# Softmax sums of the second layer's attention: quarters added by DMA, one product with ones per pair of heads

## The chip, the cores and the metric

The kernel runs on one core of one Trainium2 chip. The metric is device time in microseconds (us), the median of the runs shown; lower is better.

## The reference

Two transformer-like layers over 8 rows of 512 tokens with 128 features, all in float32. The change touches the attention of the second layer: 16 query heads of width 64 share one key and one value head.

```python
# x: (8, 512, 128), after the second layernorm
q = (x @ Wq + bq).reshape(B, S, H, DK)            # H = 16, DK = 64
k = x @ Wk + bk
v = x @ Wv + bv
scores = einsum('bshd,btd->bhst', q, k) / sqrt(DK)
w = softmax(scores, axis=-1)                      # over the 512 keys
out = einsum('bhst,btd->bshd', w, v).reshape(B, S, H * DV)
attn = out @ Wo + bo
```

Beside it stand, for each row, a first layer (an attention without softmax, and a feed-forward layer quantised to 4 bits) and a mixture of 8 experts, two for each token.

## The kernel before, in words

The program is written engine by engine, each with its own instruction list and explicit semaphores. The order comes from one list of steps, `steps`, which every engine walks. A row of the input is 64 steps of kind "o": a step is one head's scores against one quarter (128) of the keys, for all 512 queries. Heads go in pairs: eight steps make a pair, with the two heads in turn (steps 0 and 1: quarter 0 of both heads; 2 and 3: quarter 1; and so on), so a row has 8 pairs and the run 64. In the last row the 23 expert tiles (kind "ye") stand between them.

In one step TensorE (PE) makes the transposed scores with two products (`first`, L1438 and L1439) into one of two PSUM banks, and ScalarE (ACT) exponentiates them into one of the `WIDE = 6` buffers of `wide` (L846). `first` of step g waits for the exponential of step g - 2, and an exponential waits until the buffer of six steps ago has been used. Two steps after every fourth step `values` (L1449) takes four such buffers: eight products with the values (L1466), in four column tiles of 32 that run beside each other, and four with a matrix of ones (L1477), which add the weights over the 128 keys of a partition; a column tile is 32 output partitions. Float32 products are two instructions each in the trace, so a call of `values` is 16 instructions at L1466 and 8 at L1477. The last two pairs of the run are "direct": their sums are made on all 128 partitions and inverted from PSUM.

After a pair, ACT copies the values out of PSUM (`raw`, L872) and the sums (`sraw`, L877). SyncE (SP) stores the sums of the two heads and two halves to DRAM, loads them spread over 128 partitions (`sums`), VectorE (DVE) adds the two halves and inverts them (L1210), and SP stores the inverses and loads them spread over the partitions (`inv`, L500). DVE multiplies (L1223, at the steps in `NORM_AT`), and PE projects (L1498).

Around this the other work stands at fixed steps: per step DVE takes maxima of scores of pairs to come (L1029), PE makes those scores (L1392), DVE rounds queries (L1021), and the first layer of the next row runs by `L0_AT` and `L0_DVE`. The negated maxima reach the queries by a small DMA from ACT (L786), which the first scores of the next pair wait for. SP copies each pair's queries, SBUF to SBUF, with four DMAs (L537). GpSimd (POOL) has little to do in a row: three inverse roots for the layernorms (L636, each waits for DVE), the zeroing of the next row's slots in `x_rows` (L666) and the scattering of the row's tokens (L680, eight indirect DMAs).

Of the kernel before, what the change touches and what calls it, by code (L numbers as in the profile page):

```python
# [72 lines left out]
def two_layers(nc, a, out):  # L73
# [44 lines left out]
    WO_AT = [ATT - 10, ATT + 18]  # L118
# [6 lines left out]
    L0_DVE = [-14, -11, -11, -10, -7, -6, -4, -2, 0, 0, 9, 10, 13, 17, 18, 21, 25, 26, 29, 30, 30, 31, 32,  # L125
              34, 35, 37, 38, 39, 40, 42, 43, 44, 44]
# [9 lines left out]
    SPLIT_STEPS = [6 + 3 * j for j in range(2 * E)]  # L136

# [27 lines left out]

    def y_of(st):
        return HC * st.t + st.m
# [10 lines left out]
    def pair_end(st, after):  # L178

        past = behind(st, BEHIND + after)  # L180
        if past is None or past.kind != "o" or past.k % PAIR != PAIR - 1:
            return None
        return past.r * (H // 2) + past.k // PAIR

# [56 lines left out]
    def norm_at(r):  # L241

        at_ = dict(enumerate(NORM_AT))
# [57 lines left out]
    with ctx:  # L301
# [54 lines left out]
        part_h = sb("part_h", [P, PARTS, S], F32R)  # L356
# [10 lines left out]
        gcmp, geq = sb("gcmp", [P, TT * E, E]), sb("geq", [P, TT * E, E])  # L367
# [7 lines left out]
        tb_nt, tb_cum, tb_big = sb("tb_nt", [1, 2, E]), sb("tb_cum", [1, E]), sb("tb_big", [1, 2, TILES, E])  # L375
        tb_sq = sb("tb_sq", [1, E, E])
# [9 lines left out]
        zeros = part_h[:].rearrange("p n s -> p (n s)")[:, 0:TT * ROW].bitcast(F32)  # L386
# [15 lines left out]
        lo_done, second_done = sem("lo_done"), sem("second_done")  # L402
        out_free = [sem(f"out_free{i}") for i in range(OUTB)]
# [56 lines left out]
        def _(sp):  # L460
# [42 lines left out]
            def sums_and_inverses(r, k):  # L503
                for p in range(H // 2):
# [4 lines left out]
                    if k == PAIR * p + 12:  # L509
# [3 lines left out]
                        sp.dma_start(scratch_s[:, 2 * (p % 2):2 * (p % 2) + 2, :].rearrange("a b n -> b a n"), sraw[0:P:TILE, p % 2, :])\  # L513
                          .then_inc(sums_stored[p % 2], 16)
                    if k == PAIR * p + 12 and p % 2 == 1:
# [3 lines left out]
                        sp.dma_start(sums[:], scratch_s.rearrange("a g (p n) -> (g p) a n", p=32)).then_inc(sums_loaded, 16)  # L519
                    if k == PAIR * p + 17 and p % 2 == 1:  # L520
# [6 lines left out]
                        load_inverse(pair)  # L527

# [42 lines left out]
            for st in steps:  # L571
                for event in head_events(st):
# [39 lines left out]
        def _(pool):  # L612
# [44 lines left out]
            pool.memset(part_h[:].bitcast(F32), 0.0).then_inc(consts, 1)  # L657
# [3 lines left out]
            def zero(n):  # L661
                if n == 0:
                    pool.wait_ge(consts, N_CONSTS)
                    pool.dma_start(x_rows[E * ZONE:, :].rearrange("(p i) c -> p (i c)", p=P), zeros).then_inc(zeroed[0], 16)
                for e in range(E):
                    pool.dma_start(x_rows[ZONE * e + S * n:ZONE * e + S * (n + 1), :].rearrange("(p i) c -> p (i c)", p=P),  # L666
                                   zeros).then_inc(zeroed[n % 2], 16)

            def scatter(n):
                for b in range(2):  # L670
# [8 lines left out]
                    for i in range(TT):  # L679
                        pool.indirect_dma_start(x_rows, bass.IndirectOffsetOnAxis(ap=slot_u[:, b, i:i + 1], axis=0),  # L680
                                                xr[:, i, :], None).then_inc(scattered, 16)

            root()
            root()
            zero(0)
            zero(1)
            root()
            scatter(0)
            for j in range(2 * E):
                if SPLIT_STEPS[j] in (27, 45):  # L690
                    root()
# [4 lines left out]
            for n in range(1, NB):  # L696
                if n > 1:
                    root()
                    root()
# [887 lines left out]
```

## Time and profile before

| | us |
|---|---|
| median of 3 runs | 1349.38 (1345.81 to 1350.87) |
| profiled execution, its own time | 1346.94 |
| its span, first to last instruction | 1345.2 |

| engine | busy us | share |
|---|---|---|
| PE (matmul) | 1233.3 | 92% |
| DVE | 1011.2 | 75% |
| ACT | 683.2 | 51% |
| POOL | 263.2 | 20% |

The span has a beginning of 110 us, seven rows of second-layer attention from there to 1054.8 us, and the last row with the experts. Busy time of PE overlaps itself, since products run beside each other and their ends are modelled, so the chain of waits says more than the share. A line number (L1466) is one of the kernel before.

### The profile page before, as it was taken

The page shows a single profiled execution, that of the slowest core. Times are in us where ns is not written, and L with a number is a line of the kernel's source. Part 1 is how long each engine was busy: PE and PEld are TensorE (multiplying, and loading weights), DVE is VectorE, ACT ScalarE, POOL GpSimd, SP SyncE. Part 2 cuts the span into 40 slices and gives each one's busy share as a digit, 9 for nine tenths or more (in the row PEclk, how much of TensorE's full clock was granted, in tenths as well). Part 3 has the DMA queues.
Part 4 walks back from the last instruction along what each step waited for, and adds up shares of the span by engine and source line. Part 5 has one row for each costly group of instructions (what it writes and reads, how often), then busy time and mean ns, then how long its engine had stood idle before and what let it go on. Part 6 is the DMA issues. An engine that isn't in the chain of part 4 may idle for free.

```text
span 1345.2 us, 21825 instructions
## 1 busy us (share of the span) xinstructions
PE 1233.3 (92%) x7185; PEld 725.0 (54%) x7185; DVE 1011.2 (75%) x2393; ACT 683.2 (51%) x1252; POOL 263.2 (20%) x314
## 2 busy tenths in 40 slices
PE   4559999999999999999999999999999989998997
PEld 2335445554555455555555555455555458785843
DVE  7776888578857885788588857886796767686775
ACT  3126545544554455444644464446444468685741
POOL 2033222200120012001200120012000206372640
PEclk9659999999999999999999999999999999998998
DMA  2062665122312231224222321232121457474461
GB/s 78 0 174 69 193 200 179 49 63 56 115 36 63 65 116 38 52 67 100 64 50 55 115 65 50 49 120 65 50 50 49 131 173 232 153 238 137 150 214 55
DMA packets 89779, 133.80 MB, mean 99 GB/s; under 512 B 33293, under 2 KB 49229, under 8 KB 85701
## 3 DMA queue, kind: packets, MB, share of 16 engines
q1 hardware_dynamic: 75108, 99.80, 26.2%
q0 software_dynamic: 11344, 31.64, 7.1%
q8 instruction: 59, 0.97, 0.3%
q10 hardware_dynamic: 3216, 0.97, 0.3%
q14 instruction: 52, 0.42, 0.1%
HBM read 59.86 MB, written 38.68 MB: 73 GB/s over the span
## 4 chain that ended last, share of the span: by engine, by line
PE 69%; DVE 19%; issue 4%; ACT 3%; SPq 3%; DMA 2%; POOL 1%; DVEq 0%; ACTq 0%; POOLq 0%
PE bank L1466 14%; PE bank L1438 7%; PE bank L1477 6%; PE bank L1392 6%; PE bank L1439 5%; PE bank L1297 4%; PE bank L1498 4%; PE bank L1299 4%; PE bank L1298 4%; DVE mneg L1029 4%; DVE q_lm L1021 3%; PE bank L1313 2%; PE bank L1348 2%; PE bank L1303 2%; PE bank L1356 1%
## 5 line engine op out<-in xcount | busy, mean ns | idle before, releaser
L846 ACT ACTIVATE wide<-bank 128x512 f32<-128x512 f32 x512 | 294.9, 598 | 338.2 <-PE bank L1439 337.8
L1029 DVE TENSOR_REDUCE mneg<-bank 128x1 f32<-128x512 f32 x512 | 329.7, 684 | 136.0 <-PE bank L1392 130.8
L1466 PE MATMUL bank<-wide,v_w 128*32 128x512 f32 x2048 | 246.2, 598 | 1.3 <-issue 1.0
L1438 PE MATMUL bank<-q_hh,k_hl 128*128 128x512 f32 x512 | 233.0, 455 | 11.3 <-ACT wide L846 11.3
L1439 PE MATMUL bank<-q_lm,k_h 65*128 65x512 f32 x512 | 203.1, 397 | 0.0
L1438 PEld LDWEIGHTS bank<-q_hh,k_hl 128*128 128x128 f32 x512 | 96.3, 188 | 131.6 <-issue 76.9
L636 POOL TENSOR_TENSOR rs<-rs,power 128x4 f32<-128x4 f32 x24 | 24.5, 1020 | 640.2 <-DVE rs L920 640.1
L1477 PE MATMUL bank<-wide,ones 128*32 128x512 f32 x992 | 129.1, 592 | 0.0
L708 POOL DMA_INDIRECT y_rows<-y_m,to_u x92 | 98.9, 1075 | 126.8 <-DVE y_m L1155 102.3
L1466 PEld LDWEIGHTS bank<-wide,v_w 128*32 128x32 f32 x2048 | 53.5, 109 | 121.0 <-issue 112.1
L1392 PE MATMUL bank<-k_b,q_x 128*128 128x512 f32 x256 | 104.4, 408 | 9.7 <-ACT qk L742 6.2
L1392 PE MATMUL bank<-k_a,q_x 128*128 128x512 f32 x256 | 107.1, 418 | 5.9 <-ACT hqt L766 2.6
L1021 DVE SCALAR_TENSOR_TENSOR q_lm<-bank,bq,q_x 64x512 fp32r<-64x512 f32 x128 | 95.6, 747 | 12.2 <-issue 10.8
L1439 PEld LDWEIGHTS bank<-q_lm,k_h 65*128 65x128 f32 x512 | 97.2, 190 | 11.3 <-issue 1.4
L680 POOL DMA_INDIRECT x_rows<-xr,slot_u x64 | 64.5, 1008 | 173.8 <-DVE slot_u L1101 138.0
L872 ACT ACTIVATE raw<-bank 128x512 f32<-128x512 f32 x64 | 38.2, 597 | 101.4 <-PE bank L1477 92.2
L1263 DVE TENSOR_TENSOR part_l<-wide,part_h 128x512 fp32r<-128x512 f32 x92 | 62.1, 692 | 32.9 <-ACT wide L851 32.5
L851 ACT ACTIVATE part_h<-bank,b_t 128x512 fp32r<-128x512 f32 x92 | 63.4, 689 | 35.6 <-PE bank L1299 30.3
L1477 PEld LDWEIGHTS bank<-wide,ones 128*32 128x32 f32 x992 | 32.2, 110 | 74.2 <-issue 74.2
L1498 PE MATMUL bank<-wo,on 128*128 128x128 f32 x512 | 61.8, 280 | 4.8 <-DVE on L1223 4.8
L1498 PEld LDWEIGHTS bank<-wo,on 128*128 128x128 f32 x512 | 61.2, 196 | 7.5 <-DVE on L1223 6.2
L1392 PEld LDWEIGHTS bank<-k_a,q_x 128*128 128x128 f32 x256 | 48.9, 191 | 29.3 <-ACT q_x L776 12.4
(238 smaller groups left out, 1969.8 us busy)
## 6 DMA issues: line engine op xcount, KB each, us to landing
q_hh<-q_x SPq DMA_DIRECT2D x256, 128.0 KB, 2.4
w_t<-w_rows SPq DMA_DIRECT2D x23, 1024.0 KB, 4.7
x_rows<-part_h POOLq DMA_DIRECT2D x65, 258.0 KB, 5.0
inv<-inverse_scratch SPq DMA_DIRECT2D x124, 128.0 KB, 2.9
w_rows<-w_t SPq DMA_DIRECT2D x8, 1024.0 KB, 5.0
x_m<-x_rows SPq DMA_DIRECT2D x23, 258.0 KB, 3.9
stage<-in_L_ffn_W SPq DMA_DIRECT2D x16, 256.0 KB, 5.0
yab<-y_rows POOLq DMA_DIRECT2D x8, 512.0 KB, 7.9
```

The source lines that it names most:

```text
L680: pool.indirect_dma_start(x_rows, bass.IndirectOffsetOnAxis(ap=slot_u[:, b, i:i + 1], axis=0), xr[:, i, :], None).then_inc(scattered, 16)
L708: pool.indirect_dma_start(y_rows, bass.IndirectOffsetOnAxis(ap=to_u[:, t % TO, i:i + 1], axis=0), y_m[:, t % YM, i, :], None).then_inc(y_s ...
L846: act.activation(wide[:, st.g % WIDE, :], ps, ACT.Exp, scale=SCALE1).then_inc(wide_full, 1)
L851: ins = act.activation(dst, ps, ACT.Gelu_apprx_tanh, bias=b_t[:, st.t % WT, st.m:st.m + 1])
L1021: ins = dve.scalar_tensor_tensor(q_lm[0:DK, gh % HEADS, :], ps[rows, :], bq[rows, h:h + 1], q_x[rows, pair % 2, :].bitcast(F32), ALU.add, ...
L1029: dve.tensor_reduce(mneg[:, pair % 2, col:col + 1], ps[:], X, ALU.max, negate=True).then_inc(free, 1)
L1392: into(("mx", 2 * pair + b, j), lambda ps: pe.matmul(ps[:], q_x[:, pair % 2, P * j:P * j + P], keys[:, n % 2, :], start=True, stop=True))
L1438: pe.matmul(ps, k_hl[:, n, t], q_hh[:, gh % HEADS, :], start=True, stop=False)
L1439: last = pe.matmul(ps, k_h1[0:DK + 1, n, t], q_lm[0:DK + 1, gh % HEADS, :], start=False, stop=True)
L1466: pe.matmul(ps_out[0][rows, :], v_w[:, n, c, TILE * d:TILE * d + TILE], weights, start=(c == 0), stop=(c == TT - 1))
L1477: last = pe.matmul(ps_out[1][rows, :], ones[:], weights, start=(half == 0), stop=(half == 1))
L1498: last = pe.matmul(ps[:, P * i:P * i + P], on[:, g % (H // 4), P * i:P * i + P], wo[:, g, :], start=(g == pairs.start), stop=(g == pairs.s ...
```

## The change

The products with ones are made on a sum of the four quarters instead of on each quarter, for the first 54 pairs (`ADDED`: all pairs but the last two of row 6, and those of row 7).

- SP copies the two buffers of quarter 0 of a pair (both heads, 128 x 1024 float32, 512 KB) to one of two buffers `total` (`copy_first`), at step 2 of the pair.
- POOL adds the buffers of quarters 1, 2 and 3 onto it with one accumulating DMA each (`add`, 512 KB), at steps 4, 6 and 8 (`ADD_AT`). Each waits for its two exponentials, for the copy or the add before it to have landed.
- An exponential waits in addition until the copy or add that reads its buffer has landed. `wide` still has six buffers.
- PE makes four products of 256 columns with ones on `total`, in four column tiles (2 heads x 2 halves of the queries), just ahead of the first `values` of the next pair (`sum_of_added`).
- The sums then need no addition of two halves. Their copy, stores, loads and the multiplications stand two steps later (`SUM_LATER`), and the second part of the projection two steps later (`WO_AT`).
- POOL's list is now walked by steps too: roots at steps 30, 42, 51, the eight scattering DMAs at steps 3 to 9 and 17 to 23, the zeroing at steps 25 to 39. `zeros` has a buffer of its own, `total` lies over `part_h`, and some small tables share memory.

```diff
+    ADDED = (NB - 1) * (H // 2) - 2
+    ADD_AT = {4: 1, 6: 2, 8: 3}
+    SUM_LATER = 2
+    WO_AT = [ATT - 10, ATT + 20]
...
+    ROOT_AT = [30, 42, 51]
+    SCATTER_AT = [[3, 5, 7, 9], [17, 19, 21, 23]]
+    ZERO_AT = [25 + 2 * e for e in range(E)]
...
+            def copy_first(pair):
+                g = ATT * (pair // (H // 2)) + PAIR * (pair % (H // 2))
+                sp.wait_ge(wide_full, g + 2)
+                if pair >= 2:
+                    sp.wait_ge(summed, pair - 1)
+                sp.dma_start(total[:, pair % 2], wide[:, wide_at[g]:wide_at[g] + 2, :]).then_inc(first_copied, 16)
...
+            def add(pair, c):
+                g = ATT * (pair // (H // 2)) + PAIR * (pair % (H // 2))
+                pool.wait_ge(wide_full, g + 2 * c + 2)
+                if c == 1:
+                    pool.wait_ge(first_copied, (pair + 1) * 16)
+                if pair or c > 1:
+                    pool.wait_ge(add_done, adds_before(pair, c - 1) * 16)
+                i = wide_at[g + 2 * c]
+                pool.dma_start(total[:, pair % 2], wide[:, i:i + 2, :], accum_op=ALU.add).then_inc(add_done, 16)
...
-                    if st.g >= WIDE:
-                        act.wait_ge(second_done, st.g - WIDE + 1)
+                    past = wide_before.get(st.g)
+                    if past is not None:
+                        act.wait_ge(second_done, past.g + 1)
+                        if on_sum(past):
+                            act.wait_ge(first_copied, (pair_of(past) + 1) * 16)
+                        if past.kind == "o" and added(pair_of(past)) and not on_sum(past):
+                            act.wait_ge(add_done, adds_before(pair_of(past), head_at(past.k)[1]) * 16)
...
+                pair = pair_end(st, 4)
+                if pair is not None and added(pair):
+                    act.wait_ge(summed, pair + 1)
+                    act.wait_ge(sums_stored[pair % 2], 16 * (pair // 2))
+                    act.activation(sraw[:, pair % 2, 0:S // 2], ps_out[1][:, 0:S // 2], ACT.Identity).then_inc(out_free[1], 1)
...
+            def sum_of_added(pair):
+                free_bank(("ps", pair))
+                pe.wait_ge(add_done, adds_before(pair, TT - 1) * 16)
+                for b in range(2):
+                    for h in range(2):
+                        rows, cols = slice(DK * b + TILE * h, DK * b + TILE * h + TILE), slice(S // 2 * h, S // 2 * h + S // 2)
+                        last = pe.matmul(ps_out[1][rows, 0:S // 2], ones[:], total[:, pair % 2, b, cols], start=True, stop=True)
+                last.then_inc(summed, 1)
```

On PE, at the first `values` of a pair near the end of a row, the order before is (`wide,v_w` are the products with the values, `wide,ones` those with ones):

```order
377 L1438 MATMUL bank<-q_hh,k_hl 128x512 [waits wide_full]
378 L1439 MATMUL bank<-q_lm,k_h 128x512
379 L1397 MATMUL bank<-ident,mneg 8x128 [waits small_free0,small_free3]
380 L1466 MATMUL bank<-wide,v_w 32x512 [waits wide_full,out_free1,out_free0]
381 L1466 MATMUL bank<-wide,v_w 32x512 x7
382 L1477 MATMUL bank<-wide,ones 32x512 x4
383 L1438 MATMUL bank<-q_hh,k_hl 128x512 [waits wide_full]
```

and after the change, at the same place (`total` holds the sum of the pair before):

```order
375 L1535 MATMUL bank<-q_hh,k_hl 128x512 [waits wide_full]
376 L1536 MATMUL bank<-q_lm,k_h 128x512
377 L1494 MATMUL bank<-ident,mneg 8x128 [waits small_free0,small_free3]
378 L1558 MATMUL bank<-total,ones 32x256 [waits add_done,out_free1]
379 L1558 MATMUL bank<-total,ones 32x256 x3
380 L1581 MATMUL bank<-wide,v_w 32x512 [waits wide_full,out_free0]
381 L1581 MATMUL bank<-wide,v_w 32x512 x7
382 L1535 MATMUL bank<-q_hh,k_hl 128x512 [waits wide_full]
```

The four products with ones after the values are gone, here and at the second call of the pair, and four of half the width stand ahead of the values, behind a wait for the last add.

On POOL, the work of a row before is (`rs` are the roots, `x_rows` the zeroing and scattering):

```order
L636 TENSOR_TENSOR rs<-rs,power 128x4 [waits var_set] x3
L666 DMA x_rows<-part_h 128x516 x8
L673 IOTA xr 128x4 [waits scattered]
L680 DMA x_rows<-xr,slot_u 33280x129 [waits routed,zeroed0,numbered]
L680 DMA x_rows<-xr,slot_u 33280x129 x3
```

and after the change, a stretch of the middle of a row:

```order
110 L761 DMA total<-wide 128x1024 [waits add_done,wide_full]
111 L729 DMA x_rows<-zeros 128x516 x2
112 L761 DMA total<-wide 128x1024 [waits add_done,first_copied,wide_full]
113 L729 DMA x_rows<-zeros 128x516
114 L703 TENSOR_TENSOR rs<-rs,power 128x4 [waits var_set]
115 L761 DMA total<-wide 128x1024 [waits add_done,wide_full]
116 L729 DMA x_rows<-zeros 128x516
117 L761 DMA total<-wide 128x1024 [waits add_done,wide_full]
```

Every add (L761) waits for the one before it, and zeroing, scattering and roots stand between the adds.

## Rows read from the trace of the kernel before

**Rows 1.** The page: busy time by engine; DMA queues with packets, MB and share.
```profile
PE 1233.3 (92%) x7185; PEld 725.0 (54%) x7185; DVE 1011.2 (75%) x2393; ACT 683.2 (51%) x1252; POOL 263.2 (20%) x314
q1 hardware_dynamic: 75108, 99.80, 26.2%
q0 software_dynamic: 11344, 31.64, 7.1%
```

**Rows 2.** Windows, a row and its pairs: length, busy by engine, PE clock, DMA share, GB/s.
```profile
517.10:535.30 18.20, 17.56 (x109) 10.39 (x109) 7.27 (x12) 11.42 (x21) 3.29 (x3) 1.00 0.19 46
535.30:548.80 13.50, 13.27 (x80) 6.54 (x79) 12.01 (x26) 6.37 (x14) 0.00 (x0) 1.00 0.29 80
...
580.10:596.40 16.30, 15.49 (x97) 8.30 (x95) 15.70 (x35) 7.18 (x17) 1.04 (x1) 1.00 0.16 35
...
517.10:654.10 137.00, 131.28 (x802) 73.24 (x802) 104.63 (x257) 68.51 (x129) 15.97 (x21) 1.00 0.28 70
...
791.10:928.10 137.00, 131.23 (x802) 73.23 (x801) 104.65 (x257) 68.48 (x129) 14.86 (x19) 1.00 0.25 69
```

**Rows 3.** Chain of waits, 517.10 to 654.10: shares by line, then start us, length us, what.
```profile
by line: PE bank L1466 17.6%; PE bank L1438 8.2%; PE bank L1477 8.1%; PE bank L1392 7.7%; PE bank L1439 6.5%; PE bank L1498 5.2%; DVE mneg L1029 5.0%; DVE q_lm L1021 4.3%; issue 3.5%; PE bank L1313 2.2%; PE bank L1348 1.9%; PE bank L1297 1.
...
536.76 1.85 PE bank L1466 x16
538.62 0.86 PE bank L1477 x8
...
549.17 0.59 PE bank L1362 x2
...
553.27 0.43 PE bank L1438
...
575.10 1.85 PE bank L1466 x16
...
590.64 1.29 DVE mneg L1029 x2
...
622.39 1.85 PE bank L1466 x16
```

**Rows 4.** ACT in order of time, 534.5 to 563: start us, us, instruction, idle before.
```profile
542.39 1.09 ACT L846 ACTIVATE wide<-bank 128x512 f32<-128x512 f32 x2
...
544.58 0.66 ACTq L786 DMA_DIRECT2D q_lm<-mrow  x1
547.31 0.60 ACT L846 ACTIVATE wide<-bank 128x512 f32<-128x512 f32 x1 [2.76 <-PE bank L1439]
548.24 1.09 ACT L846 ACTIVATE wide<-bank 128x512 f32<-128x512 f32 x2 [0.34 <-PE bank L1439]
...
559.17 1.08 ACT L846 ACTIVATE wide<-bank 128x512 f32<-128x512 f32 x2 [2.87 <-PE bank L1439]
```

**Rows 5.** DMA issues: what, queue, count, KB each, median us from issue to landing.
```profile
q_hh<-q_x SPq DMA_DIRECT2D x256, 128.0 KB, 2.4
w_t<-w_rows SPq DMA_DIRECT2D x23, 1024.0 KB, 4.7
```

**Rows 6.** The 512 KB loads of yab, issued by POOL: time to landing.
```profile
DMA to landing us min/median/max: 4.5/7.9/10.2
```

**Rows 7.** POOL in order of time: start us, us, instruction, idle before.
```profile
517.35 1.37 POOL L680 DMA_INDIRECT x_rows<-xr,slot_u  x1 [0.30 <-issue]
519.03 0.96 POOL L680 DMA_INDIRECT x_rows<-xr,slot_u  x1 [0.30 <-issue]
...
605.77 1.01 POOL L636 TENSOR_TENSOR rs<-rs,power 128x4 f32<-128x4 f32 x1 [24.44 <-DVE rs L920]
624.23 1.01 POOL L636 TENSOR_TENSOR rs<-rs,power 128x4 f32<-128x4 f32 x1 [17.45 <-DVE rs L920]
```

**Rows 8.** Waits of the whole run: who waited for whom, us, times, longest.
```profile
ACT wide L846 <- PE bank L1439: 337.8, 256, 4.7
```

More of the change, by code:

```diff
@@ L124, in two_layers @@
     L0_SLOTS = 29
[L125 to L126 removed]
+    L0_DVE = [-14, -13, -11, -10, -7, -6, -4, -2, 0, 0, 9, 10, 13, 17, 18, 21, 25, 26, 29, 30, 30, 32, 32,
+              34, 35, 37, 38, 39, 40, 42, 42, 44, 44]
     X_LOAD_AT = 45
@@ L164, in last_step, with pair_of, added, on_sum @@
         return g_of[r, PAIR * (h // 2) + PAIR - 2 + h % 2]
+    def pair_of(st):
+        return st.r * (H // 2) + st.k // PAIR
+    def added(pair):
+        return pair < ADDED
+    def on_sum(st):
+        return st.kind == "o" and added(pair_of(st)) and head_at(st.k)[1] == 0
+    wide_at, wide_before, users = {}, {}, [None] * WIDE
+    for st in steps:
+        if st.kind in ("o", "ye"):
+            i = len(wide_at) % WIDE
+            wide_at[st.g], wide_before[st.g] = i, users[i]
+            users[i] = st
+    def adds_before(pair, c):
+        return (TT - 1) * pair + c
     def y_of(st):
@@ L183, in pair_end, with add_event @@
         return past.r * (H // 2) + past.k // PAIR
+    def add_event(st):
+        if st.kind != "o":
+            return None
+        for at_, c in ADD_AT.items():
+            pair, s = divmod(ATT * st.r + st.k - at_, PAIR)
+            if s == 0 and 0 <= pair and added(pair):
+                return pair, c
+        return None
     def direct(pair):
@@ L241, in norm_at @@
     def norm_at(r):
-        at_ = dict(enumerate(NORM_AT))
+        at_ = {p: k + (SUM_LATER if added(r * (H // 2) + p) else 0) for p, k in enumerate(NORM_AT)}
         if r == NB - 1:
@@ L508, in sums_and_inverses @@
                         continue
-                    if k == PAIR * p + 12:
+                    later = SUM_LATER if added(pair) else 0
+                    if k == PAIR * p + 12 + later:
                         emptied(sp, ("ps", pair))
@@ L518, in sums_and_inverses @@
                         sp.wait_ge(inverted, four)
-                        sp.dma_start(sums[:], scratch_s.rearrange("a g (p n) -> (g p) a n", p=32)).then_inc(sums_loaded, 16)
-                    if k == PAIR * p + 17 and p % 2 == 1:
+                        if added(pair):
+                            sp.dma_start(sums[:, 0, :], scratch_s[0].rearrange("g (p n) -> (g p) n", p=32)).then_inc(sums_loaded, 16)
+                        else:
+                            sp.dma_start(sums[:], scratch_s.rearrange("a g (p n) -> (g p) a n", p=32)).then_inc(sums_loaded, 16)
+                    if k == PAIR * p + 17 + later and p % 2 == 1:
                         for i in range(2):
@@ L571, in _ @@
             for st in steps:
+                if st.kind == "o" and st.k % PAIR == 2 and added(pair_of(st)):
+                    copy_first(pair_of(st))
                 for event in head_events(st):
@@ L1206, in row_end @@
                     pair = r * (H // 2) + p
-                    if k == PAIR * p + 16 and not direct(pair):
+                    if k == PAIR * p + 16 + (SUM_LATER if added(pair) else 0) and not direct(pair):
                         dve.wait_ge(sums_loaded, 16 * (pair // 2 + 1))
-                        link(dve.tensor_tensor(sums[:, 0, :], sums[:, 0, :], sums[:, 1, :], ALU.add))
+                        if not added(pair):
+                            link(dve.tensor_tensor(sums[:, 0, :], sums[:, 0, :], sums[:, 1, :], ALU.add))
                         dve.reciprocal(sums[:, 0, :], sums[:, 0, :]).then_inc(inverted, 1)
@@ L1447, in first, with free_bank @@
                 last.then_inc(first_full, 1)
+            def free_bank(name):
+                b, uses = out_place[name]
+                if uses:
+                    pe.wait_ge(out_free[b], uses)
+            def sum_of_added(pair):
[6 more added lines that the diff above has]
+                last.then_inc(summed, 1)
             def values(st):
                 n, half = st.r % 2, st.k % PAIR // TT
-                pair = st.r * (H // 2) + st.k // PAIR
+                pair = pair_of(st)
                 if half == 0:
-                    for name in (("pv", pair), ("ps", pair)):
-                        b, uses = out_place[name]
-                        if uses:
-                            pe.wait_ge(out_free[b], uses)
+                    if pair and added(pair - 1):
+                        sum_of_added(pair - 1)
+                    free_bank(("pv", pair))
                     if st.k == TT - 1:
```

123 lines of the change are left out of this document (75 added, 48 removed).

## Prediction

> **What bounds the kernel now.** First the page's busy time: PE 92%, DVE 75%, ACT 51%, POOL 20% [rows 1]. That makes PE the suspect, though busy time counts products that run beside each other twice. Then one row of the input in windows: the row from 517.10 and the one from 791.10, two rows on, have the same length and busy times, so one stands for all, and its pairs show where there is room. In 137.0 us DVE is busy for 104.6, ACT for 68.5, POOL for 16.0; pair 1 (535.3 to 548.8) has DVE at 12.0 of 13.5 us, pair 4 (580.1 to 596.4) at 15.7 of 16.3 [rows 2]. The chain of waits in that row says what ends last: it is PE's nearly everywhere, with a DVE stretch from about 587 to 613 us and one after 626; the products with ones (L1477) hold 8.1% of it, the values 17.6%, the maxima on DVE 5.0% [rows 3]. ACT waits for PE's scores for 337.8 us of the run [rows 8]. So PE binds, with DVE close behind in two places, and an edit that takes work from PE pays as far as nothing new is waited for.
>
> **PE: removed and added.** A call of the products with ones takes 0.86 us on the chain [rows 3], two calls a pair. The chain of a row holds 8.1% of 137 us = 11.1 us of them [rows 3], that is 13 of the 16 calls; the other three lie where DVE is last. Added: four products of 256 columns, eight instructions in four column tiles. Not in the trace in this form. At most it costs what a call of four with 512 columns costs, 0.86; at least nothing, if it fills a wait. Time goes with columns: two instructions of 352 columns take 0.59 [rows 3], 0.295 each, against 0.86 / 4 = 0.215 for a group of four instructions that run beside each other at 512, where one product's two instructions cost 0.43. So I take half of 0.86, 0.43 a pair, and expect no change of tile shape to be paid, as the values follow in the same shape. A row has 8 such sums, 7 of them on the chain: 3.0 us. PE's part is 11.1 - 3.0 = 8.1 us a row. Where PE gives way DVE is next: pair 4 has 0.6 us to give, not 1.3 [rows 2], and the stretch from 587 to 613 stays. I leave 1.6 of the 8.1 to DVE if nothing else is late: 6.5 us a row. 54 pairs are 6.75 rows: 44 us.
>
> **ACT, DVE and the sums.** ACT's copy of sums is 256 columns instead of 512; DVE loses one short addition of 16 columns for every two pairs; both are worth nothing, since ACT has 68.5 of 137 us of work [rows 2] and the addition is a fraction of a us, eight hundredths of a row's DVE time at the very most. The sums are made a pair later on PE and used two steps later, so DVE's multiplication has less room before ACT wants `raw` again. Two steps are some 4 us; I put it at 0, and up to 1 us a row against.
>
> **The copy and the adds.** This is the unknown. 54 copies and 162 adds of 512 KB, none in the trace. What they must meet, read from ACT's order: the exponentials of quarter 1 of pair 1 are done at 542.39 + 0.60 = 543.0, and the buffer is wanted by the first exponential of pair 2 at 548.7 (the second of the two from 548.24) [rows 4], 5.7 us later. ACT may be late there: PE asks for that exponential only at 553.27 [rows 3], so the add has 553.3 - 0.6 - 543.0 = 9.7 us. One add alone should make it. The trouble is the series: each waits for the landing of the one before, three a pair. Call c the time from one add's release to the next one's.
>
> Bounds for c. Below: 128 KB, SBUF to SBUF, lands in 2.4 us [rows 5]; with the 0.3 us in front of POOL's next issue [rows 7], 2.7. Above: POOL's 512 KB loads of `yab` land in 4.5 us at least, 7.9 in the middle of a queue, 10.2 at most [rows 6]: 10.5. An add reads two times 512 KB, and the nearest row in bytes is the 1024 KB of `w_t`, 4.7 us [rows 5]. 4.7 + 0.3 = 5.0, and 0.1 for sharing the engines: c = 5.1.
>
> The Trainium skill ("Collectives: The Full Stack", The bandwidth ceiling) says that an adding DMA reads two sources through one queue and so moves about half of what a copy does. By this an add is priced like 1024 KB, which is the row that I took; no run so far shows an add.
>
> What c costs. The queue of adds can fall behind from quarter 1 of pair 2, ready at 559.17 + 0.60 = 559.8 [rows 4], to PE's sum of pair 5, ahead of the values at 622.39 [rows 3]: 62.6 us for 12 adds. In this stretch PE loses 8 calls (6.9 us) and gets 4 sums (1.7), so 57.4 remain, 4.8 for each add. A row then stalls for 12c - 57.4: at 5.1, 3.8 us, at the PE wait for the last add of a pair. The stall hides DVE's 1.6. A row gains 8.1 - 3.8 = 4.3 us; 6.75 rows, 29 us. The gain is gone at 12c = 65.5, c = 5.46.
>
> POOL's other work: two roots come late, released by DVE at 605.77 and 624.23 [rows 7], and an add behind them is late with them. Both stand in pairs of over 15 us; I count nothing. The scattering DMAs, 0.96 to 1.37 us each [rows 7], and the zeroing are issued while an add is in flight, so POOL has time, but their packets share the engines.
>
> The Trainium skill ("SBUF — State Buffer", the box on the trap "DVE blocks DMA") says that descriptors of POOL's DMAs wait while DVE runs an instruction that uses both port pairs. It speaks against the change, as all adds are POOL's. The scatters' 0.96 against 1.37 [rows 7] may be that; if each add paid 0.4 us more, c would be 5.5 and the gain 0.
>
> **Sum.** The profiled execution took 1346.9 us, 1.7 more than its span of 1345.2; its time is 2.4 below the median of 1349.4. 1346.9 - 29 + 2.4 = 1320 us on the scale of the median.
>
> **The rivals.**
> *The adds are hidden.* If c is 4.9 or less, as 4.7 for 1024 KB allows with the second read beside the first, nothing is waited for but DVE: 44 us, 1305. Against it: the DMA engines are no longer idle. It shares the forecast's side; I give it 0.15.
> *The adds become the bound (slower).* The place is PE's wait for the last add of a pair, the price c, the point from which it decides 5.46. For it: POOL's own 512 KB take 4.5 us at the least [rows 6]; a second read at the rate of POOL's queue (31.64 MB in 7.1% of 1345 us, 331 GB/s [rows 1]) is 0.52 / 331 = 1.6 us more; with 0.3 that is c = 6.4. And the engines: in a row 8 copies and 24 double reads are 56 x 0.52 = 29.4 MB, 89 us at this rate, beside the 0.28 x 137 = 38 us that they do now [rows 2], 127 of some 133. Against it: `yab` comes from DRAM in short pieces. With c = 5.9, the middle of 5.46 and 6.4, pair 1 is in it too: 15 adds in 622.4 - 543.0 = 79.4 less 6.4, 73.0, a stall of 88.5 - 73.0 = 15.5, so 7.4 us a row lost, 50 us: 1400. With 6.4 it is 23 - 8.1 = 14.9 a row, 1450. Chance 0.41.
> *No change.* c about 5.4, or another small transfer is late: the row with the maxima is issued at 544.58 and awaited by the next pair's scores within 4 us [rows 4]; half a us more for each pair in a full DMA queue is 54 x 0.5 = 27 us, all of the forecast. 1347 to 1352. Chance 0.09.
> The forecast itself has 0.35.
>
> **How the numbers follow.** What a measurement of this kernel can tell from no change is 0.5%, about 7 us. Faster by more: 0.35 + 0.15 = 0.50. Within: 0.09. Slower by more: 0.41. The likeliest single case is the forecast's side, 1320; c from 4.9 to 5.3 gives its own range of 1303 to 1338. The range for 8 in 10 takes in the case without change and half of the slower one: 1290 (PE's whole 8.1 us a row, 55 us, would be 1295) to 1405.
>
> **What would show it.** Right: at the values lines only 8 sum instructions a pair, about 0.43 us on the chain; adds landing in 4.7 to 4.9 us; pairs 2 to 5 of a row between 15 and 15.6 us, with PE waiting for the DMA into `total` for a few us in a row; rows of 131 to 134 us. Wrong: adds landing in over 5.2 us, pairs of a row all of one length three times c, a DMA share above 0.9, rows longer than 137 us; or no wait for `total` at all and DVE last. The forecast falls if the engines' sharing alone lifts c past 5.46, or if ACT waits for `total` rather than PE, which would move the stall to another place of the pair.

## The result, and the profile after

The changed kernel takes 1451.99 us (1445.2 to 1453.24, 4 runs) against 1348.24 (1345.81 to 1350.87, 4 runs): a ratio of 1.0759, 95% interval 1.0718 to 1.08. It is 104 us slower where 29 us of gain were forecast, and slower than the forecast's range of 1290 to 1405 us. The page of the changed kernel, its lines that answer to [rows 1] and the groups that the change touches:

```profile
PE 1225.4 (84%) x6753; PEld 741.1 (51%) x6753; DVE 1006.7 (69%) x2366; ACT 681.4 (47%) x1252; POOL 411.4 (28%) x476
...
q0 software_dynamic: 34672, 116.58, 36.9%
q1 hardware_dynamic: 79536, 127.68, 28.7%
...
PE 47%; DMA 29%; DVE 11%; SPq 5%; issue 5%; ACT 2%; POOL 0%; POOLq 0%; ACTq 0%; DVEq 0%
DMA total<-wide 16%; PE bank L1581 7%; PE bank L1535 4%; DMA inv<-inverse_scratch 4%; PE bank L1618 4%; DMA inverse_scratch<-sums 4%; PE bank L1489 4%; PE bank L1536 4%; PE bank L1396 4%; PE bank L1394 4%; PE bank L1395 3%; DMA q_lm<-mrow 3%; SPq L602 3%; DVE mneg L1125 2%; PE bank L1410 2%
...
L761 POOL DMA_DIRECT2D total<-wide x162 | 142.6, 880 | 677.0 <-DMA total<-wide 395.6
...
L1320 DVE TENSOR_TENSOR on<-raw,inv 128x512 f32<-128x512 f32 x62 | 42.6, 687 | 101.1 <-DMA inv<-inverse_scratch 100.6
```

PE is busy for 8 us less than before and ends 106 us later: the loss is waiting, not work. The DMA engines, at 7.1% and 26.2% for the two main queues before [rows 1], are now at 36.9 and 28.7%, and DMA holds 29% of the chain that ended last. Beside the adds (`total`) the chain has the stores and the loads of the inverted sums (`inverse_scratch`, `inv`) and the maxima (`q_lm`), transfers of the same size as before. A window over row 3, which answers to the rows of 137.0 us in [rows 2]:

```profile
560.90:712.20 151.30, 128.73 (x737) 75.02 (x737) 104.30 (x252) 68.34 (x130) 37.53 (x45) 0.93 0.73 173
```

A row takes 151 us instead of 137.0; PE is busy for 128.7 instead of 131.3, the DMA share is 0.73 instead of 0.28, and the granted clock 0.93 instead of 1.00. Row 0 is worse: from its first exponential to the next row's it takes 171.3 us against 133.0. From there to row 7 the rows are 151.0, 149.2, 152.9, 151.3, 149.0 and 129.3 us, against five of 137.0 and one of 126.7. Row 7 with the experts, from its first exponential to the end of the span, takes 289.3 us against 290.4. The chain of waits in this window (start us, us, what), with the DMA pieces and those that answer to [rows 3]:

```profile
by line: PE bank L1581 9.8%; DMA inv<-inverse_scratch 7.7%; DMA inverse_scratch<-sums 7.3%; DMA total<-wide 7.1%; DMA q_lm<-mrow 7.0%; PE bank L1535 6.2%; PE bank L1489 5.8%; PE bank L1536 5.1%; PE bank L1618 4.7%; issue 4.1%; DVE q_lm L111
...
569.23 0.57 PE bank L1558 x8
...
599.92 5.65 DMA total<-wide
...
606.92 5.07 DMA q_lm<-mrow
...
641.60 6.75 DMA inverse_scratch<-sums
...
648.88 5.74 DMA inv<-inverse_scratch
...
664.95 5.58 DMA q_lm<-mrow
...
679.89 4.29 DMA inverse_scratch<-sums
...
685.98 5.91 DMA inv<-inverse_scratch
```

PE's products on `total` are there: 0.57 us for eight instructions ahead of the values, where 0.43 was forecast. But 7.7 + 7.3 + 7.1 + 7.0% of the row, 44 us, are four kinds of DMA, of which the adds are only the third. In the chain of before no DMA stood in the row. What a small transfer waits for is seen in SP's own order. Before (start us, us, what):

```profile
537.39 0.34 SPq L524 DMA_DIRECT2D inverse_scratch<-sums  x1
538.81 2.40 SPq L500 DMA_DIRECT2D inv<-inverse_scratch  x4
542.04 2.41 SPq L537 DMA_DIRECT2D q_hh<-q_x  x4
```

and after:

```profile
638.23 3.26 SPq L602 DMA_DIRECT2D q_hh<-q_x  x4
641.60 0.54 SPq L581 DMA_DIRECT2D inverse_scratch<-sums  x1
648.36 2.24 SPq L548 DMA_DIRECT2D inv<-inverse_scratch  x2
```

Before, the 8 KB of inverses were stored from 537.39 and the load that waits for them was issued at 538.81, 1.4 us later; the four query copies came behind. After, DVE has the inverses ready at 638.1 (L1307), but the four query copies, whose issue takes 3.3 us, stand ahead of the store, and from the store to the load it is 6.8 us instead of 1.4. Both things are new: the order in SP's queue, and the time that the same bytes take. The maxima show the second alone. ACT issued them at 606.92. The DMA queues from there to 610.0 (packets, MB, share of 16 engines):

```profile
q0 software_dynamic: 125, 0.51, 82.9%
```

and from 610.05 to 610.2:

```profile
q10 hardware_dynamic: 14, 0.00, 14.5%
```

In the first 3.1 us q10, ACT's queue, has no packet, while q0, POOL's, fills 82.9% of all engines with one add. Then 14 of its 16 packets come within 0.15 us, just as the add ends on nearly all engines; the other two start at 611.07, as the last piece of the add ends. PE's scores began at 612.13, 5.2 us after the issue. Before, the maxima were issued at 544.58 [rows 4]. Their 16 packets were through within 2 us (544.6 to 546.6), beside query copies on q1, and PE's first scores of the next pair began 3.5 us after the issue without a wait:

```profile
q1 hardware_dynamic: 152, 0.24, 53.0%
q10 hardware_dynamic: 16, 0.00, 1.0%
...
548.04 0.42 PE L1438 MATMUL bank<-q_hh,k_hl 128*128 128x512 f32 x1
```

The Trainium skill ("DMA: Bandwidth & Descriptors", Queues, rings and completion order) says that an engine drains a whole packet of some 9 to 17 descriptors from one queue before it goes to the next. The trace agrees: the page's q0 has 34672 - 11344 = 23328 packets more than before, 144 for each of 162 adds or nine for each engine, and in the stretch above ACT's queue is served when they are through.

The waits for DMA in the whole run (us, times, longest), which answer to [rows 8]:

```profile
DVE on L1320 <- DMA inv<-inverse_scratch: 100.6, 23, 9.5
...
ACT wide L934 <- DMA total<-wide: 94.1, 44, 7.4
...
PE bank L1535 <- DMA q_lm<-mrow: 45.4, 28, 3.0
...
PE bank L1558 <- DMA total<-wide: 39.4, 23, 6.5
```

Before, DVE's group at L1223 waited for `inv` for 8.8 us in all. PE and ACT wait for the adds for 94.1 + 39.4 = 133.5 us together. POOL in order of time, an answer to [rows 7]:

```profile
594.35 0.88 POOL L761 DMA_DIRECT2D total<-wide  x1 [3.80 <-ACT wide L934]
...
599.92 0.86 POOL L761 DMA_DIRECT2D total<-wide  x1 [3.35 <-DMA total<-wide]
...
606.13 0.87 POOL L761 DMA_DIRECT2D total<-wide  x1 [4.01 <-DMA total<-wide]
```

c, the time from one add to the next that waits for it, is 5.6 and 6.2 us here (the next is 6.1) where 5.1 was forecast. In row 0 the adds are nearly the whole chain (window 110 to 250 us, its shares and its longest piece):

```profile
by line: DMA total<-wide 74.9%; issue 5.6%; DMA stage<-in_L_ffn_W 4.5%; PE bank L1581 3.4%; SPq L602 1.6%; PE bank L1558 1.5%; ACT wide L934 1.3%; PE bank L1535 1.2%; POOL x_rows L742 1.0%; PE bank L1489 0.9%; POOL w_t L749 0.9%; PE bank L1
...
199.78 9.51 DMA total<-wide
```

SP's 16 loads of weights (256 KB each) and 8 stores of 1024 KB stand in the same stretch, and one add takes up to 9.5 us from issue to landing.

### The profile page after: what moved, and what is told of

It is laid out like the page before. It is cut to its first block, busy times and chain, and to the rows that moved or that the text cites. A ratio compares the mean times of both kernels' runs of the same rounds, so it can differ in the third digit from the quotient of the medians.

```text
span 1451.5 us, 21412 instructions
## 1 busy us (share of the span) xinstructions
PE 1225.4 (84%) x6753; PEld 741.1 (51%) x6753; DVE 1006.7 (69%) x2366; ACT 681.4 (47%) x1252; POOL 411.4 (28%) x476
## 3 DMA queue, kind: packets, MB, share of 16 engines
q0 software_dynamic: 34672, 116.58, 36.9%
q1 hardware_dynamic: 79536, 127.68, 28.7%
## 4 chain that ended last, share of the span: by engine, by line
PE 47%; DMA 29%; DVE 11%; SPq 5%; issue 5%; ACT 2%; POOL 0%; POOLq 0%; ACTq 0%; DVEq 0%
DMA total<-wide 16%; PE bank L1581 7%; PE bank L1535 4%; DMA inv<-inverse_scratch 4%; PE bank L1618 4%; DMA inverse_scratch<-sums 4%; PE bank L1489 4%; PE bank L1536 4%; PE bank L1396 4%; PE bank L1394 4%; PE bank L1395 3%; DMA q_lm<-mrow 3%; SPq L602 3%; DVE mneg L1125 2%; PE bank L1410 2%
## 5 line engine op out<-in xcount | busy, mean ns | idle before, releaser
L761 POOL DMA_DIRECT2D total<-wide x162 | 142.6, 880 | 677.0 <-DMA total<-wide 395.6
L1535 PE MATMUL bank<-q_hh,k_hl 128*128 128x512 f32 x512 | 243.0, 475 | 54.9 <-DMA q_lm<-mrow 45.4
L1581 PE MATMUL bank<-wide,v_w 128*32 128x512 f32 x2048 | 265.8, 638 | 0.3 <-issue 0.3
L1536 PE MATMUL bank<-q_lm,k_h 65*128 65x512 f32 x512 | 210.7, 412 | 0.0
L1535 PEld LDWEIGHTS bank<-q_hh,k_hl 128*128 128x128 f32 x512 | 101.6, 198 | 183.2 <-issue 121.1
L1581 PEld LDWEIGHTS bank<-wide,v_w 128*32 128x32 f32 x2048 | 65.0, 116 | 124.1 <-issue 109.4
L1320 DVE TENSOR_TENSOR on<-raw,inv 128x512 f32<-128x512 f32 x62 | 42.6, 687 | 101.1 <-DMA inv<-inverse_scratch 100.6
L1536 PEld LDWEIGHTS bank<-q_lm,k_h 65*128 65x128 f32 x512 | 102.5, 200 | 12.8 <-issue 1.9
L1558 PE MATMUL bank<-total,ones 128*32 128x256 f32 x432 | 38.0, 425 | 39.5 <-DMA total<-wide 39.4
L1489 PEld LDWEIGHTS bank<-k_b,q_x 128*128 128x128 f32 x256 | 51.6, 201 | 32.8 <-DVE mneg L1125 13.0
```

The costliest lines, as they stand in the source:

```text
L761: pool.dma_start(total[:, pair % 2], wide[:, i:i + 2, :], accum_op=ALU.add).then_inc(add_done, 16)
L1489: into(("mx", 2 * pair + b, j), lambda ps: pe.matmul(ps[:], q_x[:, pair % 2, P * j:P * j + P], keys[:, n % 2, :], start=True, stop=True))
L1535: pe.matmul(ps, k_hl[:, n, t], q_hh[:, gh % HEADS, :], start=True, stop=False)
L1536: last = pe.matmul(ps, k_h1[0:DK + 1, n, t], q_lm[0:DK + 1, gh % HEADS, :], start=False, stop=True)
L1581: last = pe.matmul(ps_out[0][rows, :], v_w[:, n, c, TILE * d:TILE * d + TILE], weights_of(c, b), start=(c == 0), stop=(c == TT - 1))
```

## The experiments

Times are medians beside runs of the kernel before on the same chip, the ratio has its 95% interval. The experiments ran on three chips, and only the ratios are compared between them. "Row" is the length of rows 1 to 5, from one row's first exponential to the next row's. e2, e3, e5, e7, e9 and e10 leave out part of the computation; the change, e1, e4, e6, e8, e11 and e12 are whole.

| run | ratio | row, us |
|---|---|---|
| the change | 1.0759 [1.0718, 1.08] | 149 to 153 |
| e1, order alone | 1.0017 [0.9996, 1.0039] | 136 |
| e2, 64 columns | 1.0003 [0.9968, 1.0039] | 134 to 141 |
| e3, ACT and PE don't wait for adds | 1.0613 [1.0578, 1.0649] | 145 to 153 |
| e4, adds by POOL | 1.1004 [1.0971, 1.1036] | 154 to 157 |
| e5, 64 columns, queries later | 0.9681 [0.9645, 0.9718] | 128 to 131 |
| e6, the change, queries later | 1.0732 [1.0673, 1.0791] | 145 to 150 |
| e7, copies instead of adds | 1.0359 [1.0291, 1.0427] | 141 to 143 |
| e8, each add in two | 1.3666 [1.3607, 1.3724] | 206 to 210 |
| e9, as e3, queries later | 1.0498 [1.0451, 1.0546] | 143 to 147 |
| e10, 256 columns, queries later | 0.9918 [0.9889, 0.9948] | 130 to 134 |
| e11, adds in half of the pairs | 1.0705 [1.0659, 1.0752] | 148 to 150 |
| e12, e6 with maxima sent earlier | 1.0645 [1.0599, 1.0691] | 147 to 150 |

**e1: the order alone.**

```diff
-    ADDED = (NB - 1) * (H // 2) - 2
+    ADDED = 0
```

> ADDED = 0: every pair makes its sums by products on the quarters as before, with no copy and no add; the new order on POOL, the shifted entries of L0_DVE, WO_AT + 2 and the new memory places stay. Theory L (load: the added DMAs fill the engines, and the small transfers behind them, maxima, inverses, come late): 1345 to 1353. Theory S (series: the exponentials and PE wait for the chain of adds): the same, 1345 to 1353. Theory O (order: the moved work on POOL and DVE costs it): 1400 or more.

1358.72 us against 1357.29. Everything that is not an add (POOL's list by steps, the memory layout, the later steps of the projection) costs nothing that can be told in the whole run; rows 1 to 5 are 1.2 us shorter than before (135.8 against 137.0), row 0 is 5.7 us longer. The two steps of `SUM_LATER` hold for pairs with adds alone, so e1 does not have them.

**e2: an eighth of the bytes.** The copy and the adds move 64 of the 512 query columns; the rest of `total` stays one. Their number, waits and order are the same.

```diff
-sp.dma_start(total[:, pair % 2], wide[:, wide_at[g]:wide_at[g] + 2, :])
+sp.dma_start(total[:, pair % 2, :, 0:64], wide[:, wide_at[g]:wide_at[g] + 2, 0:64])
-pool.dma_start(total[:, pair % 2], wide[:, i:i + 2, :], accum_op=ALU.add)
+pool.dma_start(total[:, pair % 2, :, 0:64], wide[:, i:i + 2, 0:64], accum_op=ALU.add)
```

> Copy and adds move 64 of each 512 columns, an eighth of the bytes, with all their waits; the sums of the other columns are of a constant, so that part of the computation is left out. L and S both: the adds land in 2.5 to 3 us, nothing is late, and PE's gain is seen: 1300 to 1315. If waits and issue of 216 more DMAs cost by themselves, whatever they move: 1345 or more.

1357.92 us against 1357.29. This is in the range of the third forecast, the one for waits and issue that cost by themselves; e5 tells what it was. Beside the change's 1.0759 all of the loss is gone with seven eighths of the bytes. So the bytes are what makes the kernel slow; but the gain did not come either. The chain in a stretch of one row:

```profile
541.62 1.90 SPq L602
543.63 2.04 DMA inverse_scratch<-sums
...
546.19 3.15 DMA inv<-inverse_scratch
```

The inverses are still last, here and two more times in the stretch, and each time the query copies (L602) stand just ahead of their store.

**e3: the load of the adds, and neither ACT nor PE waits for it.** Copy and adds read a constant tile, PE's sum reads it too, and neither ACT nor PE waits for an add. SP's list still does: each copy waits there for an add of the pair before.

```diff
-pool.dma_start(total[:, pair % 2], wide[:, i:i + 2, :], accum_op=ALU.add)
+pool.dma_start(total[:, pair % 2], wo[:].rearrange("p (b g) f -> p b (g f)", b=2), accum_op=ALU.add)
...
-                pe.wait_ge(add_done, adds_before(pair, TT - 1) * 16)
```

> The same copies and adds of 512 KB at the same steps, but their source is the constant tile wo, and PE's products with ones read wo: no exponential and no product waits for them any more (the sums are not the softmax's, that part is left out). S: the loss is gone and PE's gain is seen, 1300 to 1320. L: the small transfers are as late as with the change, 1400 to 1440, with inverse_scratch, inv and q_lm in the chain.

1440.59 us: 6.1 of the 7.6% remain with no wait for an add on ACT and PE. This refutes the rival of the prediction as it was put (PE's wait for the last add), although that rival named nearly the right time. DVE's wait for the inverses:

```profile
DVE on L1321 <- DMA inv<-inverse_scratch: 119.1, 24, 9.0
```

**e4: POOL adds instead of its DMAs.** No copy by SP; the first add reads two buffers of `wide`.

```diff
-pool.dma_start(total[:, pair % 2], wide[:, i:i + 2, :], accum_op=ALU.add).then_inc(add_done, 16)
+into = total[:, pair % 2]
+pool.tensor_tensor(into, wide[:, j:j + 2, :] if c == 1 else into, wide[:, i:i + 2, :], ALU.add).then_inc(add_done, 1)
```

> No copy and no adding DMA: POOL itself adds the quarters with three 128x1024 tensor_tensor of some 2.6 us each (from its 1.32 us for 512 columns), same waits, same products on PE. L and S: DMA is as before, POOL has room (8 of 16 us a pair), 1300 to 1320. If DVE and POOL hinder each other at SBUF, DVE's two-input instructions get longer and it is 1345 or more.

1491.29 us, worse than by DMA. The page's groups (busy us, mean ns):

```profile
L760 POOL TENSOR_TENSOR total<-total,wide 128x1024 f32<-128x1024 f32 x108 | 257.5, 2384 | 198.3 <-ACT wide L931 194.8
...
L1317 DVE TENSOR_TENSOR on<-raw,inv 128x512 f32<-128x512 f32 x62 | 58.5, 944 | 17.2 <-DMA inv<-inverse_scratch 16.7
```

An add takes 2.38 us, and ACT waits for it for only 23.1 us in the run. It is DVE that pays: it holds 33% of the chain that ended last, 19% before, and is busy for 1188.6 us against 1006.7. Its multiplication takes 944 ns against 687 after the change, its additions of 352 columns 847 and 920 against 558 before, while its maxima, which read PSUM, stay at 685. The store of the inverses is behind the query copies here too, as in e2. The Trainium skill ("SBUF — State Buffer", SBUF: two separate sides) says that DVE and POOL hold their shared ports in turn, each for a whole instruction. The trace agrees in that DVE's operations on SBUF get longer beside POOL's adds, though not all of them do: one with two inputs of 352 columns (`sg<-t,qs`) stays at 525 ns.

**e5: as e2, and the query copies behind the inverses.** SP issues a pair's query copies two steps later.

```diff
-                for event in head_events(st):
-                    if event[0] == "q":
-                        copy_queries(event[1])
+                if st.kind in ("pre", "o") and st.k % PAIR == QUERY_AT + 2:
+                    late = H // 2 * st.r + st.k // PAIR + 2
+                    if 0 <= late < H // 2 * NB:
+                        copy_queries(late)
```

> e2 with one more edit: SP issues the four query copies two steps later (step 4 of a pair instead of 2), so the store of the inverses, which SUM_LATER = 2 had moved from ahead of them to behind them, is ahead of them again. Theory Q (queue: e2 kept nothing of PE's gain because the inverses come late behind the query copies on SP): the chain holds no inverse_scratch and SPq L602 and the rows fall to 129 to 132 us, 2.0 to 3.5% under the kernel before. Rival R (the round trip of the sums is too long by itself, since they are made four steps later): no change against e2, ratio 0.995 to 1.003. Sums are of an eighth of the columns, as in e2.

1310.33 us against 1355.15: 44.8 us faster. A row:

```profile
526.00:655.00 129.00, 121.44 (x739) 71.44 (x739) 104.70 (x254) 68.24 (x130) 45.87 (x46) 1.00 0.41 90
```

This is the prediction's case without a wait for the adds, 137.0 - 6.5 = 130.5 us a row and 44 in all, measured at 129.0 and 44.8. PE's part of the sum was right in size: against e1, which has the new order too, rows 1 to 5 are 6.7 us shorter in the mean, where 6.5 was forecast. That the total is hit so closely is in part luck, since rows 1 to 6 gain 6 to 9 us each and row 0 nothing (135.4 us against 133.0). The place in SP's queue is worth 3.2% between e2 and e5. The kernel before was not run with its query copies later, so what that edit alone would do there is open.

**e6: the whole change with that queue.** The same edit on the changed kernel.

> The changed kernel with that same edit, all bytes. If Q and load add up: 1.076 less some 0.02 to 0.03, 1.045 to 1.055. If load alone decides (every transfer waits for a whole add on its engine): 1.065 to 1.08.

1450.27 us: the repair that is worth 3.2% at 64 columns gives 0.3% here, within the intervals. DVE's wait for the inverses falls from 100.6 us to 38.5, and others rise:

```profile
ACT wide L935 <- DMA total<-wide: 123.9, 55, 5.9
...
PE bank L1536 <- DMA q_lm<-mrow: 59.3, 26, 4.3
...
DVE on L1321 <- DMA inv<-inverse_scratch: 38.5, 15, 6.0
```

**e7: copies instead of adds.** The same bytes to the same place, without the read of the target.

```diff
-pool.dma_start(total[:, pair % 2], wide[:, i:i + 2, :], accum_op=ALU.add).then_inc(add_done, 16)
+pool.dma_start(total[:, pair % 2], wide[:, i:i + 2, :]).then_inc(add_done, 16)
```

> The three adds of a pair are plain copies by POOL of the same bytes (the sum is of quarter 3 alone, the addition is left out), all waits kept. Their packets should take 160 ns instead of 328, engines are busy half as long. Theory L (an engine drains one whole add before it serves another queue, so a small transfer is late by up to 8 x 0.33 = 2.6 us): the delay halves, ratio 1.02 to 1.045. Theory S (the fixed part of the series' latency decides): under 1 us less for each of 24 adds a row, ratio above 1.05.

A ratio of 1.0359: about half of the loss. Its page has q0 at

```profile
q0 software_dynamic: 34672, 116.58, 22.8%
```

of a span of 1397.2 us. Over before's 7.1% of 1345.2 that is (0.228 x 1397.2 - 0.071 x 1345.2) / 162 = 1.38 us of every engine for a copy, and by the same working (36.9% of 1451.5) 2.72 us for an add: twice. The Trainium skill ("Collectives: The Full Stack", The bandwidth ceiling) puts an adding DMA at half the rate of a copy; the trace agrees.

**e8: each add as two of 64 partitions.** Meant to let small transfers in between.

```diff
-pool.dma_start(total[:, pair % 2], wide[:, i:i + 2, :], accum_op=ALU.add).then_inc(add_done, 16)
+for part in range(2):
+    here = slice(64 * part, 64 * part + 64)
+    pool.dma_start(total[here, pair % 2], wide[here, i:i + 2, :], accum_op=ALU.add).then_inc(add_done, 16)
```

> Each add is two DMAs of 64 partitions (4 descriptors on an engine instead of 8), same bytes. If an engine changes queues between DMAs, small transfers wait half as long: 1.05 to 1.065. If it drains the queue, or POOL's 24 more issues of 0.9 us a row make the series longer: 1.075 to 1.10.

1851.87 us, 1.3666, far above both forecasts. The page:

```profile
q0 software_dynamic: 37264, 116.59, 47.6%
...
DMA total<-wide 63%; POOL total L763 5%; PE bank L1398 2%; PE bank L1396 2%; PE bank L1397 2%; PE bank L1583 2%; PE bank L1402 1%; PE bank L1620 1%; PE bank L1537 1%; PE bank L1412 1%; PE bank L1538 1%; PE bank L1491 1%; ACT wide L936 1%; PE bank L1416 1%; DVE mneg L1127 0%
```

(0.476 x 1851.4 - 95.5) / 162 = 4.85 us of every engine for an add, against 2.72 in one piece. Half an add thus keeps each engine for 4.85 / 2 = 2.4 us, nearly as long as a whole one did. Here the adds are the bound: 63% of the chain. The Trainium skill ("SBUF — State Buffer", Door 1: The DMA port swizzle) has partitions 0 to 63 on half of the DMA ports; the trace agrees in size, no run tells that cause from another.

**e9: e3 with the query copies later.**

> e3 (full bytes, source and products on the constant tile wo, nobody waits for an add) with the query copies two steps later. Theory L (small transfers late behind whole adds): most of the load's price stays, 1.03 to 1.06, against 0.968 for an eighth of the bytes in e5. Theory S (what waits for the adds themselves decides): 0.965 to 0.985.

1417.47 us, 1.0498. Beside e5 (0.968) this is what the bytes cost with neither ACT nor PE waiting for them: 8.2%. Beside e6 (1.073) the waits for adds of these two add 2.3%. SP's list does wait for adds in e9:

```profile
SPq L594 <- DMA total<-wo: 120.4, 32, 8.8
```

Adds hold 9.2% of the chain of row 0 by this, and 5.3% of that of row 1, 23 us in all, so up to 1.7 of the 8.2% may be SP's waits. In rows 2 to 5 no add is in the chain, and they take 142.7 to 146.8 us against 128.1 to 130.7 in e5. There it is the load on the DMA engines alone, some 15 us a row. The load is that of the 54 copies by SP too; it was not told apart from that of the adds. Row 0 takes 162.7 us here against 135.4 in e5, where ACT waits for the loads of the weights that it works on next:

```profile
ACT w_t L903 <- DMA stage<-in_L_ffn_W: 42.8, 10, 10.6
...
DVE on L1322 <- DMA inv<-inverse_scratch: 41.4, 15, 6.4
```

**e10: half of the columns, queries later.** e5 with 256 for 64.

> e5 with 256 of 512 columns copied and added, half the bytes (the sums of the rest left out). If the price goes with the time that an add holds an engine and begins where the slack of the small transfers (1 to 3 us) is used up, half the bytes cost much less than half: 0.975 to 1.00. If it is proportional to bytes: 0.968 + (256-64)/(512-64) x 0.105 = 1.013, 1.005 to 1.025.

1337.76 us, 0.9918. Against e5 an eighth to a half of the bytes costs 2.4%, from a half to all (e6) 8.1%. Rows 1 to 5 are 130 to 134 us, row 0 is 151.6. Bytes are not the best measure, since with part of the columns the pieces are shorter: by the working of e7 (q0 at 16.3, 27.4 and 37.2% of spans of 1308.4, 1329.0 and 1447.2 us) an add keeps each engine for 0.73 us in e5, 1.66 in e10 and 2.73 in e6. Steps of 0.93 and 1.07 us cost 2.4 and 8.1%. So the loss is not in proportion to this time either. It is small at first and then steep, which fits slack that is used up first.

**e11: adds in every other two pairs.** The rest have their products with ones as before.

```diff
-        return pair < ADDED
+        return pair < ADDED and pair // 2 % 2 == 0
```

> The whole computation. Of every four pairs the first two have their sums by DMA, the other two by products as before; query copies later as in e6. Half the gain of PE (1.6%) and half the load, but at full strength where it is: if load is paid pair by pair, 1 + (1.073 - 1) / 2 = 1.037, 1.025 to 1.045. If it has to pile up over a row: 0.985 to 1.01.

1445.42 us, 1.0705, above both forecasts: with half of the adds nearly all of the loss is there. POOL's adds in one row, and ACT's waits:

```profile
655.36 0.85 POOL L766 DMA_DIRECT2D total<-wide  x1 [3.61 <-DMA total<-wide]
...
664.75 0.90 POOL L766 DMA_DIRECT2D total<-wide  x1 [6.68 <-DMA total<-wide]
670.94 0.87 POOL L766 DMA_DIRECT2D total<-wide  x1 [5.28 <-DMA total<-wide]
```

```profile
ACT wide L939 <- DMA total<-wide: 168.0, 63, 5.4
```

ACT waits for adds for 168.0 us, more than in e6 (123.9). Two pairs with six adds fall behind by themselves, since each takes 5 to 6 us (the last of a pair at 655.36, the next pair's first at 664.75 behind its copy, the next 6.2 later), where two steps of 137.0 / 32 = 4.3 us release the next. The pause in the pairs between does not pay that back, because ACT, and PE behind it, stop while it lasts. That reading is from the trace; it was not tested apart.

**e12: the maxima one step earlier.** e6, with the maxima turned and sent at step 4 of a pair instead of 5.

```diff
-        if s == TT + 1 and 0 <= here + 1 < total:
+        if s == TT and 0 <= here + 1 < total:
```

> e6, the whole computation and all bytes, with the maxima turned and sent one step earlier (step 4 of a pair instead of 5), some 2 us more of room for the small transfer that the next pair's scores wait for. Theory L: the wait for q_lm (7% of a row in the changed kernel) shrinks, 1.045 to 1.06. If another late transfer takes its place: 1.065 to 1.075.

1440.01 us, 1.0645, between the two forecasts; its interval and that of e6 overlap a little.

```profile
ACT wide L935 <- DMA total<-wide: 191.3, 77, 5.6
```

PE's wait for the maxima falls from 59.3 us to 12.7, and ACT's for the adds rises from 123.9 to 191.3. A wait that is taken away comes back as the next one.

## Why the prediction was wrong, point by point

**What bound the kernel before: right.** e5 shows it. With the products gone and few transfers late (DMAs still hold 7% of its chain) a row takes 129 us and the run 44.8 us less; the prediction had 130.5 and 44. The sums, 0.43 us a pair forecast, take 0.57 on the chain, 1 us a row. The prediction's remark beside the 0.43 misreads two rows: 0.86 / 4 = 0.215 us is one product of two instructions in a call and not a group of four instructions, and the 0.43 of L1438 is one instruction and not two. The half of 0.86 does not rest on it.

**"and 0.1 for sharing the engines", and "half a us more for each pair" for the small transfers: wrong, and this decided it.** In its sum the prediction put the crowding of the DMA engines into the adds' own time and asked only whether an add is late for its users. It is the other transfers that are late for theirs: the inverses' store 4.3 to 6.8 us on the chain, where it took 1.4, their load 5.7 to 5.9, where it took 2.9, the maxima 5.1 to 5.6, where they were in place 3.5 us after their issue. That is 2 to 5 us each and not half a one. An add keeps each engine for 2.72 us, and what another queue issues meanwhile comes behind. e9 prices it: 8.2% of the run with neither ACT nor PE waiting for an add. The rival of no change, "another small transfer is late", named the mechanism with a quarter of its price: 8.2% of 1350 us over 54 pairs is 2.0 us a pair.

**SUM_LATER, "I put it at 0, and up to 1 us a row against": wrong.** The working looked at ACT's buffers and not at SP's queue. With the sums two steps later the store of the inverses comes behind four query copies. At 64 columns that is worth 3.2% or 43 us (e2 against e5), the whole gain and about 8 us in each of rows 1 to 5; at full size it is hidden by the adds (0.3%, e6).

**c = 5.1: too low.** 5.6 to 6.2 in the middle of the run, up to 9.5 in row 0, where the loads of weights share the engines. The adds are the third of the four kinds of DMA in the chain of a row (7.1%). The waits of ACT and PE for them are worth 1.5% in the changed kernel (e3), though by their sum they are 133.5 us and `total` has 16% of its chain, and 2.3% in e6 (e9), where it has 27%.

**The rival "the adds become the bound" gave 1450 at c = 6.4, and the run took 1452; it was not right for that.** Its place, PE's wait for the last add, is 39.4 us of the run, and with the waits of ACT and PE gone the kernel is still 6.1% slower (e3). Only in row 0 are the adds nearly the whole chain, and row 0 takes 162 us without these waits as well (e3, e9). Its sum for the engines, 127 of 133 us, was too high (0.73 x 151.3 = 110 us in the trace), but the direction was right, and it should have been read as a warning for every other queue and not for the adds alone.

**POOL's issue: not stretched.** The prediction feared 0.4 us more for each add behind DVE. The 162 issues take 852 to 1062 ns, 872 in the median, with DVE busy for 69% of the span: none is 0.4 us longer than the shortest.

**The clock: not in the prediction.** The granted clock is 0.925 over the run against 0.970. In one place of row 3 the wait for the inverses ends at 691.89; PE then stands idle for 1.8 us before 694.69 and for 1.5 us before 697.60, each time for DVE, and from 696.5 the clock is at the lower level:

```profile
698.90:702.50 3.60, 3.60 (x21) 0.62 (x14) 3.31 (x19) 0.38 (x1) 0.71 (x1) 0.50 0.73 143
```

0.50 is the level of 1.2 GHz: a call of the values takes 3.41 us there, 1.85 elsewhere. So such a wait can cost more than its length. With 0.93 over the row some 14% of its 151 us ran at this level, 21 us, and at most half of that, 10 us (an estimate from the 0.93), is work that would have been done sooner. No run held the clock apart from the waits, so how much of the 14 us a row this is stays open.

**Together.** On the scale of the ratio: PE's gain -3.2% (e5), the bytes +8.2% (e9 against e5), the waits of ACT and PE for adds +2.3% (e6), the queue's order +0.3%: 1.076. These are differences from one run to the next, so they must add up; the cause of each is shown as far as said above. e5 leaves most of the sum out and e9 all of it, so neither is a version to use, and no kernel that computes everything was faster than before.

## What to carry to other kernels

Before work is moved to a DMA, list every small transfer that some engine waits for, on any queue, and add to each the time that one large transfer holds a DMA engine: the idle share of the engines did not show this delay here. When a step is moved, read the issuing engine's queue at the old and the new place. And price a wait by a run without it and not by its share of the chain: here waits for a DMA that holds 16% of the chain were worth 1.5%, since others stood right behind them.

## What the runs showed of the hardware

- An accumulating DMA of 512 KB within SBUF keeps each of 16 engines for 2.72 us, a copy of the same size 1.38; split into two of 64 partitions it is 4.85 (the change, e7, e8).
- POOL's issue of such an add takes 880 ns, and 547 without the addition. With 64 or 256 columns for 512 it is about 1.2 us (1218 ns in e2, 1214 in e10), with fewer bytes: the rows of `total` no longer lie end to end, and q0 has 55408 packets instead of 34672.
- POOL's addition of 128 x 1024 in float32 takes 2.38 us and makes DVE's multiplication of two tiles in SBUF longer by 37% (687 to 944 ns in the mean), not its maxima, which read PSUM (e4).
